# Loading a stage's weights one stage later, and moving the context stage's stores to ScalarE's queue

## The reference

```
x = x + L0_attn(layernorm(x))                    # causal, 16 heads of 16, rotary q and k
x = x + L0_xattn(layernorm(x), ctx, ctx, mask)   # keys and values from a context of 2 x 77 rows
x = x + L0_ffn(layernorm(x))                     # 8 experts, the best one per token
x = x + L1_attn(layernorm(x))                    # 16 heads of 64
x = x + L1_xattn(layernorm(x), ctx, ctx)         # again the context
x = x + L1_ffn(layernorm(x))                     # attention, then 8 experts, the best two
```

## Time and profile before

| | |
|---|---|
| profiled execution | 2861.38 us, of which the span from first to last instruction 2859.6 |
| three timed runs | 2862.38 to 2863.9 us, median 2862.62 |
| PE busy | 2420.2 us, 85% of the span |
| DVE busy | 1628.9 us, 57% |
| ACT busy | 1130.6 us, 40% |
| POOL busy | 924.2 us, 32% |
| DMA queue q1 (SP's) | 227.86 MB, 25.9% of 16 engines |
| mean granted TensorE clock | 0.896 of full speed |

### The profile page before, as it was taken

One profiled execution on the slowest core, in us unless ns is written; L12 is line 12 of the kernel. 1 busy time (PEld: TensorE's weight loads), 2 busy tenths in 40 slices (PEclk: granted clock), 3 DMA queues, 4 the chain that ended last, 5 costly groups with the idle time before them and its releaser, 6 DMA issues. The chain is left out here.

```text
span 2859.6 us, 44563 instructions
## 1 busy us (share of the span) xinstructions
PE 2420.2 (85%) x16004; PEld 1295.1 (45%) x16010; DVE 1628.9 (57%) x2579; ACT 1130.6 (40%) x2043; POOL 924.2 (32%) x740
## 2 busy tenths in 40 slices
PE   5678997866997995999999999777759999959996
PEld 4533335235886773333333332642622222248885
DVE  4778864654333334666666664246668999562223
ACT  2435664321000331444444444133426777712221
POOL 2521003311221112767767777122440000003331
PEclk8879998567998997999999999875869999969998
DMA  4432213425663555122222221442351111034555
GB/s 138 113 77 65 75 23 86 104 63 181 202 202 114 194 194 164 53 79 76 74 86 78 86 68 54 141 101 61 103 128 37 51 42 35 6 104 160 186 195 180
DMA packets 209626, 298.88 MB, mean 105 GB/s; under 512 B 51289, under 2 KB 149619, under 8 KB 208950
## 3 DMA queue, kind: packets, MB, share of 16 engines
q1 hardware_dynamic: 182326, 227.86, 25.9%
q0 software_dynamic: 22944, 63.99, 7.7%
q10 hardware_dynamic: 4192, 4.85, 0.9%
HBM read 205.03 MB, written 90.92 MB: 103 GB/s over the span
## 5 line engine op out<-in xcount | busy, mean ns | idle before, releaser
L1609 ACT ACTIVATE a_probs<-a_cols 128x512 f32<-128x512 f32 (+3 forms) x896 | 445.2, 549 | 242.8 <-PE a_cols L1539 162.9
L1631 DVE TENSOR_REDUCE a_mxw<-a_rows 128x2 f32<-128x1024 f32 (+1 forms) x448 | 475.7, 1100 | 66.7 <-PE a_rows L1497 41.6
L2058 DVE TENSOR_REDUCE a_mxw<-a_rows 128x2 f32<-128x1024 f32 x256 | 313.4, 1224 | 209.8 <-PE a_rows L1896 208.0
L2036 ACT ACTIVATE a_probs<-a_cols 128x1024 f32<-128x1024 f32 x256 | 261.7, 1024 | 268.9 <-PE a_cols L1925 253.6
L1877 POOL TENSOR_TENSOR a_sums<-a_sums,a_probs 128x1024 f32<-128x1024 f32 x128 | 309.3, 2416 | 105.7 <-ACT a_probs L2036 92.7
L1539 PE MATMUL a_cols<-a_qs,a_ks 50*128 50x512 bf16 (+7 forms) x1792 | 275.1, 363 | 14.9 <-DMA a_qs<-a_nparts 8.8
L2315 PE MATMUL e_psU<-e_xT,e_w 128*128 128x256 f32 x1216 | 271.4, 381 | 1.9 <-ACT e_xT L2362 1.2
L1921 PE MATMUL a_cols<-a_qf,a_kf 64*128 64x512 f32 x1024 | 267.9, 601 | 0.1
L1567 PE MATMUL a_out<-a_probs,a_vs 128*17 128x256 f32 (+4 forms) x3328 | 256.0, 381 | 0.2 <-ACT a_probs L1609 0.2
L1497 PE MATMUL a_rows<-a_ks,a_qs 48*128 48x512 bf16 (+3 forms) x896 | 174.7, 386 | 90.6 <-DVE a_mxw L1631 43.7
L1939 PE MATMUL a_out<-a_probs,a_vs 128*64 128x512 f32 x1024 | 248.6, 606 | 0.0
(11 more groups left out here) (274 smaller groups left out, 3295.6 us busy)
## 6 DMA issues: line engine op xcount, KB each, us to landing
e_w<-in_w SPq DMA_DIRECT2D x69, 512.0 KB
e_w<-in_w SPq DMA_DIRECT2D x30, 1024.0 KB
a_qs<-q_scratch SPq DMA_DIRECT2D x336, 64.0 KB, 2.3
qk_wide_scratch<-t_f SPq DMA_DIRECT2D x32, 512.0 KB, 2.9
q_scratch<-t_parts POOLq DMA_DIRECT2D x56, 192.0 KB, 2.6
a_ks<-k_scratch SPq DMA_DIRECT2D x144, 64.0 KB, 2.4
vw_scratch<-t_v SPq DMA_DIRECT2D x8, 1040.0 KB, 4.6
a_vs<-vw_scratch SPq DMA_DIRECT2D x16, 520.0 KB, 6.7
```

What stands on the lines that cost most here:

```text
L1609: act.activation(pr[ug % RING][:, 2 * hp + e, c0:512], psC[(2 * at + e) % 3][:, 0:512 - c0], ACT.Exp, scale=scale).then_inc(ex_done, 1)
L1631: dve.tensor_reduce(mxw[w][:, a, hp, :, t % 4:t % 4 + 1], src[:, :, 0:n], AX.X, ALU.max).then_inc(s_free, 1)
L2036: act.activation(pr[i][:], psC[i % 2][:], ACT.Exp, scale=scale).then_inc(ex_done, 1)
L2058: dve.tensor_reduce(mxw[:, j % 2, :, j // 2:j // 2 + 1], psR[:], AX.X, ALU.max).then_inc(s_free, 1)
```

## The change

The six loads of the first token stage are issued by SP in the context stage's block instead of the setup stage's. The five stores of the context stage are issued by ACT instead of SP. Nobody waits for their landing in the context stage; instead SP waits for it in the token stage, just before it issues the loads that read what was stored. The tiles that the stores read, and the semaphore of the stores, are therefore moved to the home of the token stage's weights, which outlives the context stage.

```
+class ContextParts:
+    def __init__(self, home, NL):
+        W = B * SC
+        self.keys = [home.sb(f"keys{l}", [P, KD, 3, W], BF16) for l in range(NL)]
+        self.mask = home.sb("mask", [1, HEADS // 2, W], BF16)
+        self.stored, self.n = home.sem("stored"), 16 * (NL * KD + 1)
...
-def setup_stage(nc, G, x, context, weights):
+def setup_stage(nc, G, x, context):
...
                 sp.dma_start(G["X"][:], x.rearrange("(t p) d -> p t d", p=P)).then_inc(G["x_loaded"], 16)
-                weights.load(sp)
...
                     if not back:
+                        if later_from is not None:
+                            sp.wait_ge(later_from.stored, later_from.n)
                         for dst, src, sem in later_loads:
                             sp.dma_start(dst, src).then_inc(sem, 16)
...
-        parts = [st.sb(f"parts{l}", [P, KD, 3, W], BF16) for l in range(NL)]
+        parts, mb, stored = kept.keys, kept.mask, kept.stored
...
-        mb = st.sb("mb", [1, 2 * HG, W], BF16)
-        ready, stored, done = st.sem("ready"), st.sem("stored"), st.sem("done")
+        ready, done = st.sem("ready"), st.sem("done")
...
             @block.sync
             def _(sp):
+                next_weights.load(sp)
+
+            @block.scalar
+            def _(act):
                 for l, k_out in enumerate(outs):
-                    sp.wait_ge(done, l + 1)
+                    act.wait_ge(done, l + 1)
                     for m in range(KD):
-                        sp.dma_start(k_out[:, m * P:(m + 1) * P].rearrange("i f s -> f i s"), parts[l][:, m]
-                                     ).then_inc(stored, 16)
+                        act.dma_start(k_out[:, m * P:(m + 1) * P].rearrange("i f s -> f i s"), parts[l][:, m]
+                                      ).then_inc(stored, 16)
                     if l == 0:
-                        sp.dma_start(mask_out, mb[:].rearrange("p g s -> p (g s)")).then_inc(stored, 16)
-                sp.wait_ge(stored, 16 * (NL * KD + 1))
+                        act.dma_start(mask_out, mb[:].rearrange("p g s -> p (g s)")).then_inc(stored, 16)
...
+            kept = ContextParts(w.home, 2)
...
-                setup_stage(nc, G, A["x"], cw, w)
-                context_stage(nc, G, "c", cw, CK, CM)
-            token_stage(nc, G, "t0", w, x_loaded=G["x_loaded"], norm="ln", resid=G["X"], units=units(Q16, K16), outs=V16,
+                setup_stage(nc, G, A["x"], cw)
+                context_stage(nc, G, "c", cw, kept, w, CK, CM)
+            token_stage(nc, G, "t0", w, later_from=kept, x_loaded=G["x_loaded"], norm="ln", resid=G["X"], units=units(Q16, K16), outs=V16,
```

More of the change, by code:

```diff
@@ L295, in token_stage @@
 def token_stage(nc, G, tag, weights, *, norm, attn=None, resid=None, units=(), wide=None, heads_group=4, hd=16, outs=None,
-                wide_b=None, x_loaded=None, rows_out=None, later_loads=()):
+                wide_b=None, x_loaded=None, rows_out=None, later_loads=(), later_from=None):
     has, kf, v_cols, rope = weights.has, weights.kf, weights.v_cols, weights.rope
@@ L844, in _, with context_stage @@
                 in_stages(step)
-def context_stage(nc, G, tag, weights, outs, mask_out):
+def context_stage(nc, G, tag, weights, kept, next_weights, outs, mask_out):
     W = B * SC
```

## The result

| | executions | median us | range |
|---|---|---|---|
| before, timed beside the change | 20 | 2860.16 | 2854.58 to 2870.33 |
| after | 20 | 2853.31 | 2843.9 to 2859.38 |
| profiled execution after | 1 | 2849.90 (span 2848.2) | |

Ratio 0.9974, 95% interval 0.9965 to 0.9983: faster by 0.26%, or 7.4 us (4.9 to 10.0). The three executions of before that the forecast started from (2862.38 to 2863.9) look tight; they are three of the twenty, and the twenty spread over 16 us.

A forecast was written before the change was run, and what follows sets the result against it. Bound: two early idle stretches where all engines wait for SP, issuing weights and awaiting stores. - 3.6 - 2.8 + 0.1 + 0.45 = - 5.85 us from 2862.62 gives 2856.8; own range 2855 to 2858.5, with rivals 2853 to 2860.8.

The forecast's parts named there:

- The two ends and the mechanism: Before the context and token stages all engines wait for SP: issuing weights until 13.94, then 2.8 us for stores to land.
- The landing of the context loads: Context stage start: loads ready at 11.2, so PE starts there instead of 14.81, 3.6 us earlier; bounds 6.9 and 14.8.
- The reading of the small packets: Setup loads: the last DMA packet under 512 B before a long pause, in 10.6 to 10.7, marks the context loads' landing.
- the end of the wf issue: SP's issue of weight wf came free at 11.20, as if waiting for room that the last context load gave.
- The stores: End of the context stage: the 2.8 us wait for landing goes; two ACT issues take 0.92 to 1.0, adding 0.1.
- The weights not being late: Token stage start: sin lands at 26.6, at most 29.6 beside the stores, before its first reader at 31.0; cost nothing.
- The rival: Token stage weights become the wait: sin lands at 31.6 to 34.6, losing 0.6 to 3.6; about 2859 us; chance 0.08.
- The second clearing: After the token stage, one more semaphore clearing and barrier for the weights' home: adds 0.45 us, bounds 0.3 and 0.83.
- The clock: PE's clock in the context and token stages: same states, shifted; each of two rises may move 0.7 us either way.
- The slower rival: Token stage start: clock not raised in the first chunk, 8.7 us more per slow chunk, a loss of 2.9; chance 0.03.
- The level: Whole kernel: a median after of 2856.8 us, from the 2862.62 median of three runs before, less 5.85.
- Given or taken elsewhere: Stages behind the start shift against the clock: gain under 4 or over 8 us, 2859.5 or 2854; chance 0.10.

The follow-up runs named there:

- the loads per layer: The changed kernel, but TensorE and VectorE wait for each layer's context loads apart; ratio to the kernel before 0.9959 (0.9943 to 0.9974).

## Why the prediction was right or wrong

**The two ends and the mechanism: right.** Both waits were where it put them, both went, and the token stage began at 25.72 against 25.9. POOL ended at 6.89 + 4.70 = 11.6, SP issued sin until 13.75, nobody waited for either.

**The landing of the context loads: mis-sized.** This is the term of 3.6. It measured 4.5 (14.81 - 10.30), and over the seven traces in which the ten loads and x were issued as in the change and awaited together 3.7 to 5.7 (first product at 9.13 to 11.08, mean 10.0). The reading of the small packets was right for that execution, as the nine later traces show (11.1 by it, 11.2 in the forecast); it was one execution, taken as the rule. The second support, the end of the wf issue, is no sign of the landing: it missed it by 0.8 to 1.8 us in three traces of seven. The bounds that were stated, 6.9 and 14.8, said nothing of a spread of 2 us between executions.

**The stores: the wait was there and went, with ACT's issues at 1.18 instead of 1.0.** The 2.8 is what the kernel before waited. Beside the moved weights the same landing takes longer, 24.89 to 28.55, which is 3.7 in the changed kernel and 6.2 to 6.6 where the stores are issued earliest. The forecast counted its two parts as independent; without the second, the first gave 2.8 of its 4.2. In other kernels two issues on ACT took 0.91 to 1.19. The stores landed at 28.55 (forecast 27.9). The rule of the Trainium skill that the forecast weighed ("DMA: Bandwidth & Descriptors", section "Issuing engines are not separate DMA queues") is borne out: the stores landed at 28.6 from SP's queue and at 28.5 from ACT's, and beside the weights they took 3.8 where they took 2.8. The weights were delayed less: sin landed 12.6 to 13.6 after its issue in the ten traces with both parts, 12.1 and 12.3 in the two of before. In the sum it changed nothing, because neither landing is awaited where it would count.

**The weights not being late: right.** sin landed at 13.32 + 12.6 = 25.9, 5 us ahead of its first reader. The rival fell.

**The second clearing: 0.40 for 0.45. The clock: the same states, shifted, as forecast.** From first product to first signal of DVE it is 9.5 before and 10.0 after, and 8.7 to 10.0 in all traces; the first chunk's 32 products took 10.12 and 10.01, and 8.56 with the loads per layer. That is the 0.7 either way of the forecast. The slower rival didn't come near.

**The sum: 5.85 forecast, 6.24 in the pair of traces.** The terms: - 4.5 for the start, + 0.5 for the longer context stage, + 0.3 for ACT, - 2.8 for the wait, which is 6.5 at the token stage; then - 0.1, and + 0.4 for the clearing. That the sum came so near is in part luck: the start was sized 0.9 too small, and the longer context stage and ACT's issues, 0.5 and 0.2 beyond the forecast, took most of it back. The second trace of the same kernel gave 7.58.

**The level: wrong, and the larger part of the miss.** The measured 2853.31 is 3.5 below the forecast and outside its own range of 2855 to 2858.5. The step that failed is "a median after should lie at 2862.62 - 5.85". It took the median of three executions for the kernel's time, and their spread of 1.5 us for its noise. Of 125 executions of that code the mean is 2859.2 and the standard deviation 3.8; the 20 timed beside the change had their median at 2860.16, 2.5 below the start of the sum. The other 1.0 is the difference of the two medians, 6.85, less 5.85. The interval of the ratio is 0.09% either way with twenty executions on each side; 0.2% as the mark was right in size, but a start from three executions could not carry it: their median alone strays by some 2.5 us (an estimate from the 3.8), more than the 1.75 that the forecast's own range allowed either way.

**Given or taken elsewhere: not shown either way.** The rest of the span went down by 5.2 us in the first pair of traces; the traces of other kernels with the same code there lie on both sides.

What stays open: why the rest of the span varies by 14.5 us between executions of the same code. The stages that vary most are the first attention stage (307.5 to 316.5 us) and the wide one (682.5 to 694.2). In the changed kernel's twenty executions, eight with a mean granted clock of 0.897 or more had a mean time of 2848.8, and seven with 0.894 or less 2857.4; the clock goes with the time, but which of them leads was not tried.

## What to carry to other kernels

Where stages end in a barrier, look for the engine that arrives last: issuing transfers for a later stage, and waiting for a store that nobody reads yet, both count as arriving late, and both can be moved behind the barrier. What then holds the stage is the next wait in line; here it was the landing of its own loads, and splitting that wait by what is needed first brought the stage's first product another 1.9 us or more ahead, in the one trace of it. Two waits that are moved one after the other need not add up: a transfer that is moved can make a later landing take longer, and then the wait for that landing must go, too. A gain of a few microseconds is read at a fixed point of the trace right behind the edit, and a level only from many executions.

## What the runs showed of the hardware

- An issue can last several microseconds. The load of wf, right behind that of x (2 MB), took SP 4.35 to 5.08 us in the order of before and 2.92 to 4.35 in the changed order; bf behind it took 0.6 to 1.6, the other loads nearly always 0.4 to 0.6. What the issue waits for, no run shows.
- Stores of 0.46 MB issued while 3.5 MB of weights were on their way landed between 27.83 and 28.95 in ten traces, though the last of them were issued between 20.61 and 23.71, from SP's queue or ACT's.
- Ten loads of together 1.44 MB by their shapes, issued identically in seven traces, let the first product start between 9.13 and 11.08; issued in half the time from two queues, at 10.30. In nine traces the product came 0.4 to 0.5 us behind the last DMA packet under 512 B.
- Products of zeros in 7.2 of PE's 10 us of pause kept the granted clock at 1.00. The token stage behind them lasted 101.3 us, against 103.2 to 104.6 in the traces without them.
